# Two groups of heads in half a bank, a causal mask carried by 43 contraction rows, and a feed-forward in pairs of blocks

## The chip, the cores and the metric

The kernel runs on one core of a Trainium2 chip. The time is device microseconds of one execution, the median of several. A core has TensorE (PE, matmuls into eight PSUM banks of 128 partitions x 512 fp32), VectorE (DVE), ScalarE (ACT), GpSimd (POOL, which doesn't touch PSUM) and SyncE (SP), whose queue issues every DMA here.

## The reference

One gated cross-attention layer and one gated expert layer over x of 8 batches x 256 tokens x 128 channels:

```
xn  = layernorm(x)
y   = softmax(causal(q k^T)) v + softmax(qc kc^T) vc      # 16 heads of 8 channels; kc, vc from ctx (256 x 64)
x1  = x + tanh(g_xattn) * (y Wp + bp)
xn2 = layernorm(x1)
w   = route(xn2)                                          # 4 of 16 experts, chosen in 2 of 4 groups
out = x1 + tanh(g_ffn) * sum_e w[e] * (silu(xn2 Wg_e) * (xn2 Wu_e)) Wd_e     # 64 hidden channels an expert
```

In the self-attention a query token attends to keys at or before it; the others count as minus infinity ahead of the softmax. The cross-attention has no mask.

## The kernel before, in words

All 8 batches go through the same steps, and the steps of neighbouring batches overlap. No scheduler decides at build time: `ORDERS` holds one list of words for each engine (`max:3:11` is chunk 11 of batch 3), and an engine runs its list strictly in order. What one step needs of another engine is a semaphore wait at its head.

Scores are made twice. Queries and keys are split into three bf16 parts, and stacked along the contraction: rows 0 to 71 of `q_stack` and `k_stack` give fp32-like products of one head, and row 72 (`SHIFT_ROW`) holds minus the row's maximum in `q_stack` and 1.0 in `k_stack`. The stacks are written through DRAM (`part_scr`) by DMAs of 24 rows each, three for q and three for k, of each batch and each kind (CROSS, SELF); three slots of stacks rotate.

- `max_chunk` (L704, L701): scores with queries on the partitions, 512 columns to a bank, two banks; DVE takes the maximum of each row (`take_max`, L859, 28 a batch). In SELF chunks a matmul of `ident_b` with the constant `causal` (L695) first writes 0 or -1e30 into the diagonal blocks, and the score matmuls add to it.
- `exp_chunk` (L717): scores with keys on the partitions, with the shift row, two banks; ACT writes their exponentials to `probs` (L627, 28 a batch). In SELF chunks POOL then sets the positions of later keys to 0 (`mask`, L541, 12 a batch).
- `weigh_values` (L737, `pv` in the orders): four heads side by side, each in 32 of the 128 output partitions: 8 values, a sum of weights, and 23 zero columns of `v_ext`. One group of four heads fills half of `pv_bank` (256 queries), so a kind's 16 heads fill two banks one after the other.
- `evacuate_pv` (L633, ACT) copies each full bank; PE transposes it in four 128x128 blocks (`y`, L775); `merge` (DVE, L866 and L874) divides by the sums; `add_kinds` (POOL, L548) adds the two kinds. All of this happens four times a batch, the adding twice.
- Then `yT`, `wp`, the residual, the second layernorm, `logits`, the routing (`route`, DVE, 18 small steps), and its weights transposed (`combT`), sent to DRAM and spread over all partitions by DMA (`cout`, `cin`).
- The feed-forward works in 8 blocks of 128 hidden channels. Two banks rotate, each with a block's gates in one half and its ups in the other (`gate_up`, L805, L806). ACT takes the tanh of the gates (L643), DVE makes `f_gate` (`swish`, L939) and times the ups (`times_up`, L946), POOL multiplies with the routing weights (`combine`, L555, `fhc` in the orders), and `down` (L814) adds the eight blocks up in the next bank of the two.

An fp32 matmul stands in the trace as two instructions. Ten small uses of PE share one bank, `misc`, strictly in turn.

## Time and profile before

| | us |
|---|---|
| median of 3 runs (382.36 to 383.38) | 382.51 |
| profiled execution, its own time | 381.71 |
| its span in the trace | 379.9 |
| PE busy, 3200 matmuls | 346.4 |
| DVE busy | 270.2 |
| ACT busy | 206.0 |
| POOL busy | 200.6 |

The profile page gives each engine's busy time as the union of its instructions. A matmul's interval lasts from its start until its last column is through the array, so the intervals of matmuls that follow each other overlap: what a matmul costs PE is the distance to the next one's start, read from a timeline. In a timeline several instructions in a row of the same kind are one row with their count.

```
PE   1759989999999999999999999999999989997594
DVE  2127588686898789888787778777788785566751
ACT  1321247688767645676467645864576557643020
POOL 5935031564870889079525992185704830955313
```

These are tenths of busy time in 40 slices of 9.5 us. PE is full from 60 us to 340 us. Ahead of that the first batches come through loads, splits and DMAs; behind it the last batch's routing and feed-forward stand alone.

### The profile page before, as it was taken

The numbers are of one execution on the slowest core, as the hardware profiler recorded it, in microseconds if no ns is written. First come the engines' busy times: TensorE is split into PE (matmuls) and PEld (weight loads), VectorE is DVE, ScalarE is ACT, GpSimd is POOL, SyncE is SP. The second block draws the span as 40 slices with busy tenths as digits, with TensorE's granted clock in tenths as the row PEclk, the third lists the DMA queues.
The fourth block names the chain that finished last, engine by engine and source line by source line (L and its number), as shares of the span: only waits on it lengthen the run. The fifth ranks groups of instructions, "written<-read, shape, count | busy, mean of one in ns | idle before, by whom it ended". The sixth has DMA issues, their size and how long they took to land.

```text
span 379.9 us, 8947 instructions
## 1 busy us (share of the span) xinstructions
PE 346.4 (91%) x3200; PEld 250.6 (66%) x3200; DVE 270.2 (71%) x742; ACT 206.0 (54%) x442; POOL 200.6 (53%) x304
## 2 busy tenths in 40 slices
PE   1759989999999999999999999999999989997594
PEld 0423556676777787677876788678867867865454
DVE  2127588686898789888787778777788785566751
ACT  1321247688767645676467645864576557643020
POOL 5935031564870889079525992185704830955313
PEclk9999999999999999999999999999999999999789
DMA  3265144463344742494315422644044204105060
GB/s 92 83 201 155 59 126 144 142 205 117 94 127 129 159 145 60 138 172 126 112 47 127 129 89 93 150 91 117 17 133 96 43 14 94 23 18 110 2 125 16
DMA packets 31325, 39.13 MB, mean 103 GB/s; under 512 B 2832, under 2 KB 28592, under 8 KB 28848
## 3 DMA queue, kind: packets, MB, share of 16 engines
q1 hardware_dynamic: 31280, 38.55, 37.9%
q8 instruction: 26, 0.43, 0.4%
q14 instruction: 19, 0.16, 0.1%
HBM read 30.89 MB, written 7.47 MB: 101 GB/s over the span
## 4 chain that ended last, share of the span: by engine, by line
PE 77%; DVE 8%; DMA 5%; SPq 3%; ACT 2%; issue 2%; POOL 2%; POOLq 0%; ACTq 0%
PE bank L737 13%; PE bank L717 12%; PE bank L704 8%; PE bank L805 7%; PE bank L806 6%; PE bank L814 6%; PE bank L701 5%; DMA k_stack<-part_scr 5%; PE bank L695 4%; PE bank L775 3%; PE bank L756 2%; PE bank L743 2%; SPq L444 2%; PE bank L758 1%; PE bank L765 1%
## 5 line engine op out<-in xcount | busy, mean ns | idle before, releaser
L859 DVE TENSOR_REDUCE row_max<-bank 128x2 f32<-128x512 f32 (+1 forms) x224 | 149.3, 686 | 46.4 <-PE bank L704 27.4
L627 ACT ACTIVATE probs<-bank 128x512 f32<-128x512 f32 x224 | 128.6, 596 | 54.7 <-PE bank L717 44.7
L717 PE MATMUL bank<-q_stack,k_stack 73*128 73x256 bf16 (+1 forms) x512 | 80.5, 259 | 0.4 <-ACT probs L627 0.3
L541 POOL TENSOR_SCALAR_AFFINE_SELECT probs<-probs 128x256 f32<-128x256 f32 (+1 forms) x96 | 44.7, 482 | 35.7 <-ACT probs L627 35.2
L737 PE MATMUL bank<-probs,v_ext 128*32 128x256 f32 (+1 forms) x1024 | 61.7, 358 | 0.0
L555 POOL TENSOR_TENSOR f_h<-f_h,comb 128x256 f32<-128x256 f32 x64 | 45.3, 725 | 22.1 <-DMA comb<-c_scr 11.3
L704 PE MATMUL bank<-k_stack,q_stack 72*128 72x256 bf16 x256 | 50.1, 290 | 5.4 <-DMA k_stack<-part_scr 4.0
L717 PEld LDWEIGHTS bank<-q_stack,k_stack 73*128 73x128 bf16 x512 | 42.3, 98 | 14.9 <-ACT probs L627 5.7
L396 POOL TENSOR_TENSOR rest<-proj,part 128x512 f32<-128x512 f32 x14 | 16.2, 1157 | 59.9 <-ACT part L604 59.9
L805 PE MATMUL bank<-xn2T,w_pairs_sb 128*128 128x256 f32 x128 | 40.7, 400 | 2.3 <-DVE f_h L946 1.4
L737 PEld LDWEIGHTS bank<-probs,v_ext 128*32 128x32 f32 x1024 | 26.7, 109 | 23.2 <-issue 8.9
L643 ACT ACTIVATE f_tanh<-bank 128x256 f32<-128x256 f32 x64 | 24.3, 383 | 30.7 <-PE bank L806 29.5
L814 PE MATMUL bank<-w_down,f_h 128*128 128x128 f32 x256 | 37.8, 284 | 1.7 <-DVE f_h L946 1.3
L806 PE MATMUL bank<-xn2T,w_pairs_sb 128*128 128x256 f32 x128 | 38.7, 384 | 0.0
L704 PEld LDWEIGHTS bank<-k_stack,q_stack 72*128 72x128 bf16 x256 | 22.7, 101 | 22.3 <-DVE row_max L859 10.9
L701 PE MATMUL bank<-k_stack,q_stack 72*128 72x128 bf16 x384 | 37.4, 220 | 0.0
L939 DVE SCALAR_TENSOR_TENSOR f_gate<-f_tanh,bank 128x256 f32<-128x256 f32 x64 | 26.6, 415 | 14.4 <-ACT f_tanh L643 14.4
L814 PEld LDWEIGHTS bank<-w_down,f_h 128*128 128x128 f32 x256 | 32.5, 193 | 3.9 <-DVE f_h L946 1.7
L701 PEld LDWEIGHTS bank<-k_stack,q_stack 72*128 72x128 bf16 x384 | 30.1, 98 | 6.3 <-issue 0.8
L695 PE MATMUL bank<-causal,ident_b 128*128 128x256 bf16 (+1 forms) x96 | 30.4, 316 | 2.1 <-DVE row_max L859 1.4
L806 PEld LDWEIGHTS bank<-xn2T,w_pairs_sb 128*128 128x128 f32 x128 | 24.8, 194 | 3.6
L946 DVE TENSOR_TENSOR f_h<-f_gate,bank 128x256 f32<-128x256 f32 x64 | 26.4, 416 | 1.0
(103 smaller groups left out, 431.0 us busy)
## 6 DMA issues: line engine op xcount, KB each, us to landing
q_stack<-part_scr SPq DMA_DIRECT2D x48, 192.0 KB
k_stack<-part_scr SPq DMA_DIRECT2D x48, 192.0 KB
comb<-c_scr SPq DMA_DIRECT2D x16, 512.0 KB, 6.9
part_scr<-part SPq DMA_DIRECT2D x48, 128.0 KB, 3.2
x_in<-in_x SPq DMA_DIRECT2D x8, 128.0 KB, 2.8
w_pairs_sb<-in_w_pairs SPq DMA_DIRECT2D x1, 1024.0 KB, 7.0
out<-y_out SPq DMA_DIRECT2D x8, 128.0 KB, 2.4
ctx_in<-in_ctxT SPq DMA_DIRECT2D x8, 64.0 KB, 3.5
```

What stands on the lines that cost most here:

```text
L541: nc.gpsimd.affine_select(out=p, in_=p, compare_op=ALU.is_ge, fill=0.0, base=0, pattern=[[0, nh], [1, 128]], channel_multiplier=-1).then_i ...
L555: nc.gpsimd.tensor_tensor(at, at, comb[:, j, :], ALU.mult).then_inc(f_hc_done, 1)
L627: nc.scalar.activation(probs[:, seq % NP, :], exp_bank[s % 2][:, :], ACT.Exp).then_inc(exp_done, 1)
L695: pe.matmul(ps[:, :, keys - 128:keys], ident_b[:, :], causal[:, 0:nh, :], start=True, stop=False)
L701: last = pe.matmul(ps[:, n, kt * 128:(kt + 1) * 128], q, k_stack[0:STACK, s, kind, h, kt * 128:(kt + 1) * 128], start=False, stop=n == nh ...
L704: last = pe.matmul(ps[:, n, :], q, k_stack[0:STACK, s, kind, h, :], start=n == 0, stop=n == nh - 1)
L717: last = pe.matmul(ps[:, n, :], k_stack[0:STACK + 1, b % SLOTS, kind, h, kt * 128:(kt + 1) * 128], q_stack[0:STACK + 1, b % SLOTS, kind, h ...
L737: last = pe.matmul(pv_bank[32 * n:32 * n + VW, col + q0:col + T], v_ext[:, b % 2, kind, kt, 4 * g4 + n, :], p, start=kt == 0, stop=kt == N ...
L805: pe.matmul(gu_bank[use % 2][:, 0:T], w_gate[:, e0], xn2T[:, :], start=True, stop=True)
L806: pe.matmul(gu_bank[use % 2][:, T:2 * T], w_up[:, e0], xn2T[:, :], start=True, stop=True).then_inc(gu_ready, 1)
L814: last = pe.matmul(gu_bank[use % 2][:, n * 128:(n + 1) * 128], f_h[:, j, n * 128:(n + 1) * 128], w_down[:, j, :], start=j == 0 and n == 0, ...
L859: nc.vector.tensor_reduce(row_max[:, kind, qt, h0:h0 + nh], max_bank[k % 2][:, :].rearrange("p (h k) -> p h k", h=nh), AX.X, ALU.max).then ...
```

## The change

1. **Masks.** `causal`, `ident_b`, their matmul and POOL's `mask` are gone. Rows 73 to 115 of both SELF stacks hold constants `tri_q` and `tri_k` (43 rows, three tokens to a row), whose products add at most 2^-30 in size where the key is at or before the query, and -2^22 or less where it is later (all factors are powers of two). Matmuls on a diagonal block contract over 116 rows, the others over 72 or 73 as before. For that the exponential chunks of keys 0 to 127, one matmul of 256 queries a head before, are two matmuls of 128 (L731); all other widths stay. The maxima's diagonal matmuls now also read the shift row, so each load of a SELF `q_stack` is followed by a DMA that clears it (`zero_row`). Six DMAs (`tri`) place the constants in the three slots, of 43 rows x 8 KB each.
2. **Values.** Groups 2n and 2n+1 take the even and the odd heads of the same eight. The odd group reads its 32 columns of `v_ext` 16 further left, so that its values come out in partitions 16 to 31 of each strip, where the even group adds zeros. A kind's 16 heads fill one bank. Copy, transposes, merge run twice a batch, the adding once.
3. **Feed-forward.** Gates of two blocks fill `gate_bank`, ups of two blocks `up_bank`; neither has a second one. `gates_of` waits for the swish of the pair before, `ups_of` for its product. Tanh, swish, product and combine work on 512 columns, 4 a batch instead of 8. `down` writes into `gate_bank`.
4. All five orders are written anew for these steps.

```diff
+ROW_TOKENS = 3
+ROWS = (128 + ROW_TOKENS - 1) // ROW_TOKENS
+MASKED = STACK + 1 + ROWS
+AT = (2.0 ** 40, 2.0 ** -12, 2.0 ** -64)
+FROM = (2.0 ** -70, 2.0 ** -18, 2.0 ** 34)
+LATER = 2.0 ** 92
...
     'pe': '''
-        gu:6:2 y:7:3 gu:6:3 yT:7 wp:7 gu:6:4 gu:6:5 gu:6:6 gu:6:7 xn2T:7 logits:7 down:6 down:6:1 down:6:2 down:6:3
-        down:6:4 down:6:5 down:6:6 combT:7 down:6:7 gu:7 gu:7:1 gu:7:2 gu:7:3 gu:7:4 gu:7:5 gu:7:6 gu:7:7 down:7
...
+        ga:6:1 up:6:1 yT:7 wp:7 ga:6:2 up:6:2 ga:6:3 up:6:3 xn2T:7 logits:7 down:6 down:6:1 down:6:2 down:6:3 down:6:4
+        down:6:5 down:6:6 down:6:7 combT:7 ga:7 up:7 ga:7:1 ga:7:2 up:7:1 ga:7:3 up:7:2 up:7:3 down:7 down:7:1
...
+            def place_masks(s):
+                if s == 0:
+                    sp.wait_ge(const_made, 3)
+                else:
+                    sp.wait_ge(tri_in[0], 32)
+                for st, tri in ((q_stack, tri_q), (k_stack, tri_k)):
+                    first = tri[:, 0:T].unsqueeze(1).broadcast_to([ROWS, H, T])
+                    src = first if s == 0 else st[SHIFT_ROW + 1:MASKED, 0, SELF]
+                    sp.dma_start(st[SHIFT_ROW + 1:MASKED, s, SELF], src).then_inc(tri_in[s], 16)
...
+                if kind == SELF and qk == 0:
+                    if b == 0:
+                        sp.wait_ge(const_step, 4)
+                    sp.dma_start(q_stack[SHIFT_ROW:SHIFT_ROW + 1, b % SLOTS, SELF], zero_row[:, :]).then_inc(stack_in[b % SLOTS][SELF], 16)
...
+                    nc.gpsimd.memset(at_q[:, :, c:c + 1], -AT[c]).then_inc(const_step, 1)
+                    nc.gpsimd.memset(at_k[:, :, c:c + 1], FROM[c]).then_inc(const_step, 1)
+                pool.wait_ge(const_step, 4 + 2 * ROW_TOKENS)
...
-            def mask(b, m):
-                s = CROSS_C2 + m
-                _, kt, h0, nh, q0 = S2_CHUNKS[s]
-                pool.wait_ge(exp_done, b * NC2 + s + 1)
-                p = probs[:, (b * NC2 + s) % NP, :].rearrange("p (h q) -> p h q", h=nh)[:, :, 0:128]
-                nc.gpsimd.affine_select(out=p, in_=p, compare_op=ALU.is_ge, fill=0.0, base=0,
-                                        pattern=[[0, nh], [1, 128]], channel_multiplier=-1).then_inc(mask_done, 1)
...
-                if kind == SELF:
-                    pe.matmul(ps[:, :, keys - 128:keys], ident_b[:, :], causal[:, 0:nh, :], start=True, stop=False)
                 for n in range(nh):
-                    h = h0 + n
-                    q = q_stack[0:STACK, s, kind, h, qt * 128:(qt + 1) * 128]
+                    q, key = q_stack[:, s, kind, h0 + n, qt * 128:(qt + 1) * 128], k_stack[:, s, kind, h0 + n, :]
                     if kind == SELF:
-                        for kt in range(keys // 128):
-                            last = pe.matmul(ps[:, n, kt * 128:(kt + 1) * 128], q, k_stack[0:STACK, s, kind, h, kt * 128:(kt + 1) * 128],
-                                             start=False, stop=n == nh - 1 and kt == keys // 128 - 1)
+                        for kt in range(qt + 1):
+                            rows_used = MASKED if kt == qt else STACK
+                            last = pe.matmul(ps[:, n, kt * 128:(kt + 1) * 128], q[0:rows_used], key[0:rows_used, kt * 128:(kt + 1) * 128],
+                                             start=n == 0 and kt == 0, stop=n == nh - 1 and kt == qt)
...
-                    last = pe.matmul(ps[:, n, :], k_stack[0:STACK + 1, b % SLOTS, kind, h, kt * 128:(kt + 1) * 128],
-                                     q_stack[0:STACK + 1, b % SLOTS, kind, h, q0:T], start=n == 0, stop=n == nh - 1)
+                    h = h0 + 2 * n
+                    key, q = k_stack[:, b % SLOTS, kind, h, kt * 128:(kt + 1) * 128], q_stack[:, b % SLOTS, kind, h, :]
+                    if kind == SELF:
+                        for qt in range(kt, NQ):
+                            rows_used = MASKED if kt == qt else STACK + 1
+                            last = pe.matmul(ps[:, n, qt * 128 - q0:(qt + 1) * 128 - q0], key[0:rows_used], q[0:rows_used, qt * 128:(qt + 1) * 128],
+                                             start=n == 0 and qt == kt, stop=n == nh - 1 and qt == NQ - 1)
...
-                if kind == SELF:
-                    pe.wait_ge(mask_done, b * SELF_C2 + 3 * g4 + 3)
-                if g % 2 == 0:
-                    ge(pe, pv_copied, b * 4 + g // 2)
-                col = (g % 2) * T
+                if g4 == 0:
+                    ge(pe, pv_copied, b * 2 + kind)
+                col = g4 // 2 * T
...
+                        at = h * VW - VW // 2 * (g4 % 2)
+                        last = pe.matmul(pv_bank[32 * n:32 * n + VW, col + q0:col + T],
+                                         v_ext[:, b % 2, kind, kt].rearrange("p h v -> p (h v)")[:, at:at + VW], p,
+                                         start=g4 % 2 == 0 and kt == 0, stop=g4 % 2 == 1 and kt == NQ - 1, tile_position=(0, 32 * n))
...
+            def hidden(b, j, bank_of, w):
+                for n in range(2):
+                    e0 = (2 * j + n) * 128
+                    last = pe.matmul(bank_of[:, n * T:(n + 1) * T], w[:, e0:e0 + 128], xn2T[:, :], start=True, stop=True)
+                return last
+
+            def gates_of(b, j):
                 if j == 0:
                     misc_evacuated(pe, "xn2T", b)
                     if b == 0:
                         pe.wait_ge(w_experts, 32)
-                use = b * GU_USES + j
-                ge(pe, gu_free, use - 1)
-                e0 = slice(j * 128, (j + 1) * 128)
-                pe.matmul(gu_bank[use % 2][:, 0:T], w_gate[:, e0], xn2T[:, :], start=True, stop=True)
-                pe.matmul(gu_bank[use % 2][:, T:2 * T], w_up[:, e0], xn2T[:, :], start=True, stop=True).then_inc(gu_ready, 1)
+                    ge(pe, out_made, b)
+                ge(pe, f_gate_done, b * GP + j)
+                hidden(b, j, gate_bank, w_gate).then_inc(gates_ready, 1)
+
+            def ups_of(b, j):
+                ge(pe, ups_free, b * GP + j)
+                hidden(b, j, up_bank, w_up).then_inc(ups_ready, 1)
...
             def down(b, j):
-                use = b * GU_USES + NB
                 if j == 0:
-                    pe.wait_ge(gu_free, use - 1)
-                pe.wait_ge(f_hc_done, b * NB + j + 1)
+                    pe.wait_ge(f_gate_done, b * GP + GP)
+                pe.wait_ge(f_hc_done, b * GP + j // 2 + 1)
...
-                nc.vector.scalar_tensor_tensor(out=f_gate[:, j % 2], in0=f_tanh[:, j % 2], scalar=1.0, in1=gu_bank[(b * GU_USES + j) % 2][:, 0:T],
+                dve.wait_ge(f_tanh_done, b * GP + j + 1)
+                ge(dve, ups_free, b * GP + j)
+                nc.vector.scalar_tensor_tensor(out=f_gate[:, :], in0=f_tanh[:, :], scalar=1.0, in1=gate_bank[:, :],
...
+                dve.wait_ge(ups_ready, b * GP + j + 1)
```

**The orders, place 1: PE at the first SELF maxima of batch 0.** L695 is the mask matmul, L701 (after: L711) the SELF score matmuls, L770 (L787) the transposes of `shift`, L704 (L714) CROSS maxima, L717 (L734) CROSS exponentials. Before, and then after:

```order
L760 MATMUL bank<-xnT,w_model_sb 128x256
L695 MATMUL bank<-causal,ident_b 128x512
L701 MATMUL bank<-k_stack,q_stack 128x128 x4
L695 MATMUL bank<-causal,ident_b 128x512
L701 MATMUL bank<-k_stack,q_stack 128x128 x4
L770 MATMUL bank<-ident,row_max 16x128 x2
L695 MATMUL bank<-causal,ident_b 128x512
L701 MATMUL bank<-k_stack,q_stack 128x128 x4
```

```order
L777 MATMUL bank<-xnT,w_model_sb 128x256
L714 MATMUL bank<-k_stack,q_stack 128x256 x2
L787 MATMUL bank<-ident,row_max 16x128 x2
L711 MATMUL bank<-k_stack,q_stack 128x128 x16
L734 MATMUL bank<-q_stack,k_stack 128x256 x2
L711 MATMUL bank<-k_stack,q_stack 128x128 x8
L734 MATMUL bank<-q_stack,k_stack 128x256 x6
```

The mask matmuls between the groups of four are gone, and the transposes of `shift` have moved ahead of the SELF maxima.

**Place 2: DVE from the end of batch 7's routing to the feed-forward behind it.** L931 (after: L955) makes the last routing weight, L946 (L972) is the product with the ups, L985 (L1011) writes batch 6's output, L939 (L964) is the swish. Before, and then after:

```order
L928 RECIPROCAL r_sum<-r_sum 128x2
L931 SCALAR_TENSOR_TENSOR r_w<-r_sel,gate,r_sum 128x32
L946 TENSOR_TENSOR f_h<-f_gate,bank 128x256
L985 TENSOR_TENSOR y_out<-bank,x 128x256
L939 SCALAR_TENSOR_TENSOR f_gate<-f_tanh,bank 128x256
L946 TENSOR_TENSOR f_h<-f_gate,bank 128x256
```

```order
L952 RECIPROCAL r_sum<-r_sum 128x2
L955 SCALAR_TENSOR_TENSOR r_w<-r_sel,gate,r_sum 128x32
L1011 TENSOR_TENSOR y_out<-bank,x 128x256
L964 SCALAR_TENSOR_TENSOR f_gate<-f_tanh,bank 128x512
L972 TENSOR_TENSOR f_h<-f_gate,bank 128x512
L964 SCALAR_TENSOR_TENSOR f_gate<-f_tanh,bank 128x512
```

Before, the last product of batch 6 stands behind the routing of batch 7; after, it stands ahead of it.

**Place 3: SP while batch 0's SELF stacks are loaded.** L433 (after: L440) stores parts, L444 (L451) loads stacks, L448 (L459) sets a shift row, L430 places masks, L455 clears the row. Before, and then after:

```order
L411 DMA x_in<-in_x 128x2x128 [waits res_done,xn_done,misc_ready]
L412 DMA ctx_in<-in_ctxT 64x256
L433 DMA part_scr<-part 128x2x256 [waits split_cross]
L444 DMA q_stack<-part_scr 24x1x4096 [waits part_out_self]
L444 DMA q_stack<-part_scr 24x1x4096 x2
L444 DMA k_stack<-part_scr 24x1x4096 [waits part_out_self]
L444 DMA k_stack<-part_scr 24x1x4096 x2
L444 DMA q_stack<-part_scr 24x1x4096 [waits part_out_cross]
L444 DMA q_stack<-part_scr 24x1x4096 x2
L433 DMA part_scr<-part 128x2x256 [waits split_self]
L448 DMA q_stack<-shiftT 1x16x256 [waits misc_free]
```

```order
L430 DMA q_stack<-tri_q 43x16x256 [waits const_made]
L430 DMA k_stack<-tri_k 43x16x256
L451 DMA k_stack<-part_scr 24x1x4096 [waits part_out_self]
L451 DMA k_stack<-part_scr 24x1x4096 x2
L440 DMA part_scr<-part 128x2x256 [waits split_cross]
L408 DMA x_in<-in_x 128x2x128 [waits res_done,xn_done,misc_ready]
L409 DMA ctx_in<-in_ctxT 64x256
L451 DMA q_stack<-part_scr 24x1x4096 [waits part_out_self]
L451 DMA q_stack<-part_scr 24x1x4096 x2
L455 DMA q_stack<-zero_row 1x16x256 [waits const_step]
L440 DMA part_scr<-part 128x2x256 [waits split_cross]
```

After, two mask DMAs stand ahead of batch 0's SELF keys, and one that clears the shift row follows the SELF queries; batch 1's CROSS queries, ahead of the shift row before, are not among the rows: they come behind it.

## Rows read from the trace of the kernel before

**Rows 1.** The page: busy time of each engine, and the chain that ended last

```profile
PE 346.4 (91%) x3200; PEld 250.6 (66%) x3200; DVE 270.2 (71%) x742; ACT 206.0 (54%) x442; POOL 200.6 (53%) x304
...
PE 77%; DVE 8%; DMA 5%; SPq 3%; ACT 2%; issue 2%; POOL 2%; POOLq 0%; ACTq 0%
```

**Rows 2.** Windows: from:to, length, busy (x instructions) by engine, PEclk, DMA share, GB/s

```profile
0.00:45.00 45.00, 28.37 (x84) 14.66 (x85) 16.79 (x42) 11.36 (x25) 23.43 (x34) 1.00 0.41 124
...
45.00:60.00 15.00, 13.00 (x133) 8.27 (x131) 12.87 (x21) 8.05 (x17) 3.81 (x3) 1.00 0.39 116
...
100.00:140.00 40.00, 40.00 (x421) 29.28 (x419) 34.69 (x91) 26.20 (x58) 25.16 (x36) 1.00 0.49 132
...
340.00:380.00 40.00, 27.95 (x154) 20.66 (x142) 20.73 (x69) 7.39 (x19) 14.47 (x22) 0.91 0.30 61
...
60.00:340.00 280.00, 277.09 (x2842) 207.05 (x2844) 219.84 (x612) 179.15 (x383) 158.90 (x245) 1.00 0.39 105
```

**Rows 3.** Groups by form: shapes, count | busy us, mean ns | idle before

```profile
L695 PE MATMUL bank<-causal,ident_b 128*128 128x256 bf16 x64 | 17.6, 276 | 1.5 <-DVE row_max L859 1.4
...
L695 PE MATMUL bank<-causal,ident_b 128*128 128x512 bf16 x32 | 12.7, 398 | 0.6 <-DMA k_stack<-part_scr 0.5
...
L775 PE MATMUL bank<-ident,y_raw 128*128 128x128 f32 x128 | 19.7, 276 | 0.0
```

**Rows 4.** Timeline of PE, 133.0 to 134.8 us: start us, us, what, count

```profile
133.03 0.38 PE L695 MATMUL bank<-causal,ident_b 128*128 128x512 bf16 x1
133.25 0.39 PE L701 MATMUL bank<-k_stack,q_stack 72*128 72x128 bf16 x4
133.47 0.61 PE L775 MATMUL bank<-ident,y_raw 128*128 128x128 f32 x4
133.91 0.39 PE L717 MATMUL bank<-q_stack,k_stack 73*128 73x128 bf16 x4
134.14 0.27 PE L695 MATMUL bank<-causal,ident_b 128*128 128x256 bf16 x1
134.25 0.39 PE L701 MATMUL bank<-k_stack,q_stack 72*128 72x128 bf16 x4
134.48 0.38 PE L717 MATMUL bank<-q_stack,k_stack 73*128 73x256 bf16 x2
134.70 0.27 PE L695 MATMUL bank<-causal,ident_b 128*128 128x256 bf16 x1
```

**Rows 5.** Groups by form on DVE, ACT and POOL

```profile
L859 DVE TENSOR_REDUCE row_max<-bank 128x2 f32<-128x512 f32 x192 | 127.8, 685 | 37.4 <-PE bank L704 27.4 <-PE bank L701 7.7
...
L939 DVE SCALAR_TENSOR_TENSOR f_gate<-f_tanh,bank 128x256 f32<-128x256 f32 x64 | 26.6, 415 | 14.4 <-ACT f_tanh L643 14.4
...
L946 DVE TENSOR_TENSOR f_h<-f_gate,bank 128x256 f32<-128x256 f32 x64 | 26.4, 416 | 1.0
...
L866 DVE RECIPROCAL recip<-bank 128x16 f32<-128x16 f32 x32 | 8.0, 251 | 6.6 <-PE bank L775 6.4
...
L874 DVE TENSOR_TENSOR y_self<-bank,recip 128x128 f32<-128x128 f32 x16 | 4.7, 292 | 0.6
...
L627 ACT ACTIVATE probs<-bank 128x512 f32<-128x512 f32 x224 | 128.6, 596 | 54.7 <-PE bank L717 44.7 <-PE bank L737 8.7
...
L541 POOL TENSOR_SCALAR_AFFINE_SELECT probs<-probs 128x512 f32<-128x512 f32 x32 | 20.3, 633 | 4.8 <-ACT probs L627 4.7
...
L402 POOL TENSOR_TENSOR part<-rest,part 128x512 bf16<-128x512 f32 x14 | 16.2, 1157 | 0.4
```

**Rows 6.** Timeline of the end: start us, us, what

```profile
368.51 5.51 POOL L555 TENSOR_TENSOR f_h<-f_h,comb 128x256 f32<-128x256 f32 x8 [9.18 <-DMA comb<-c_scr]
...
372.53 3.84 PE L814 MATMUL bank<-w_down,f_h 128*128 128x128 f32 x32 [1.26 <-DVE f_h L946]
...
376.40 0.42 DVE L985 TENSOR_TENSOR y_out<-bank,x 128x256 f32<-128x256 f32 x1 [3.60 <-PE bank L814]
```

**Rows 7.** Chain in order of time: a wait for a stack of batch 1

```profile
48.66 5.33 DMA k_stack<-part_scr
```

More of the change, by code:

```diff
@@ L48 @@
 for g in range(H // 4):
-    S2_CHUNKS += [(CROSS, kt, 4 * g + hp, 2, 0) for kt in range(NQ) for hp in (0, 2)]
+    S2_CHUNKS += [(CROSS, kt, first_head(g) + 2 * hp, 2, 0) for kt in range(NQ) for hp in (0, 2)]
     S2_GROUP += [g] * 4
 for g in range(H // 4):
-    S2_CHUNKS += [(SELF, 0, 4 * g, 2, 0), (SELF, 0, 4 * g + 2, 2, 0), (SELF, 1, 4 * g, 4, 128)]
+    S2_CHUNKS += [(SELF, 0, first_head(g), 2, 0), (SELF, 0, first_head(g) + 4, 2, 0), (SELF, 1, first_head(g), 4, 128)]
     S2_GROUP += [H // 4 + g] * 3
@@ L337, in build @@
         bank = [stack.enter_context(nc.psum_tensor(f"bank{n}", [128, 512], FP32)) for n in range(8)]
-        max_bank, exp_bank, pv_bank, gu_bank, misc = bank[0:2], bank[2:4], bank[4], bank[5:7], bank[7]
+        max_bank, exp_bank, pv_bank, gate_bank, up_bank, misc = bank[0:2], bank[2:4], bank[4], bank[5], bank[6], bank[7]
         w_first, w_rows, w_experts = sem("w_first"), sem("w_rows"), sem("w_experts")
@@ L343, in build @@
         const_step, const_made = sem("const_step"), sem("const_made")
+        tri_step, tri_in = sem("tri_step"), [sem(f"tri_in{s}") for s in range(SLOTS)]
         v_clear_step, v_cleared = sem("v_clear_step"), sem("v_cleared")
@@ L472, in _ @@
                     place_constants()
+                elif what == "tri":
+                    place_masks(n)
                 elif what == "experts":
@@ L490, in _ @@
             sp.wait_ge(ones_in, 16 * SLOTS)
+            for s in range(SLOTS):
+                sp.wait_ge(tri_in[s], 32)
         @block.gpsimd
@@ L573, in _ @@
                     split_step(nc.gpsimd, b, n, 2)
-                elif what == "mask":
-                    mask(b, n)
                 elif what == "yadd":
-                    add_kinds(b, n)
+                    add_kinds(b)
                 elif what == "rstd2":
@@ L688, in max_chunk @@
                     stack_here(pe, b, kind)
[L689 to L690 removed]
+                if b < SLOTS and k == CROSS_C1:
+                    pe.wait_ge(tri_in[b], 32)
                 ge(pe, max_taken, b * NC1 + k - 1)
@@ L715, in exp_chunk @@
                 for n in range(nh):
-                    h = h0 + n
-                    last = pe.matmul(ps[:, n, :], k_stack[0:STACK + 1, b % SLOTS, kind, h, kt * 128:(kt + 1) * 128],
-                                     q_stack[0:STACK + 1, b % SLOTS, kind, h, q0:T], start=n == 0, stop=n == nh - 1)
+                    h = h0 + 2 * n
[5 more added lines that the diff above has]
+                                             start=n == 0 and qt == kt, stop=n == nh - 1 and qt == NQ - 1)
+                    else:
+                        last = pe.matmul(ps[:, n, :], key[0:STACK + 1], q[0:STACK + 1], start=n == 0, stop=n == nh - 1)
                 last.then_inc(exp_scores, 1)
@@ L771, in misc_use @@
                 elif what == "y":
-                    pe.wait_ge(pv_copied, b * 4 + n + 1)
+                    pe.wait_ge(pv_copied, b * 2 + n + 1)
                     for qt in range(NQ):
-                        for g in range(2):
-                            last = pe.transpose(misc[:, (qt * 2 + g) * 128:(qt * 2 + g + 1) * 128],
-                                                y_raw[:, n % 2, g * T + qt * 128:g * T + (qt + 1) * 128], ident[:, :])
+                        for p in range(2):
+                            last = pe.transpose(misc[:, (qt * 2 + p) * 128:(qt * 2 + p + 1) * 128],
+                                                y_raw[:, n, p * T + qt * 128:p * T + (qt + 1) * 128], ident[:, :])
                 elif what == "yT":
-                    pe.wait_ge(y_added, 2 * b + 2)
+                    pe.wait_ge(y_added, b + 1)
                     last = transposes(y)
```

430 lines of the change are left out of this document (205 added, 225 removed).

## The prediction

> **What bounds the kernel now.** I read the page's busy times and its chain first, then the busy time by stage, then PE's timeline inside the full stage, and the waits of the other engines last. PE is busy for 346.4 of 379.9 us and holds 77% of the chain that ended last, DVE 8% [rows 1]. By stage it is three kernels [rows 2]. Up to 60 us the first batches' stacks are made and loaded, and PE is busy for 28 of the first 45 us and 13 of the next 15, while DVE is busy for 12.9 of those 15: it paces the maxima of batch 0. From 60 to 340 us PE is busy for 277.1 of 280 us. From 340 us on the last batch's routing and feed-forward stand alone, at a mean granted clock of 0.91, with PE busy for 28 of 40 us in short pieces between other engines.
>
> PE's busy time is a union of overlapping intervals, so I take costs from starts instead. In the piece of timeline in [rows 4] the starts follow without a hole: the mask matmul of 512 columns holds PE for 0.22 us, the one of 256 for 0.11, four score matmuls of 128 columns for 0.22 to 0.23 (0.055 each), two of 256 for 0.22 (0.11 each), four fp32 transposes for 0.44 (0.11 each). What is taken from PE's stream in the full stage is taken from the time, if nothing else is as near to its limit. DVE is the next: 34.7 of 40 us in its fullest window [rows 2]. ACT has 179 and POOL 159 of the 280.
>
> The Trainium skill ("Perfetto Trace Analysis", Identifying the Most-Contended Engine) calls matmul busy time a bad measure of how close PE is to its limit and asks for the busy share of weight loads. That share is 207.1 of 280 us here [rows 2], so by the rule PE would have room; the starts in [rows 4] say that it has none where I looked, and the measurement decides.
>
> **The change part by part.**
>
> *Mask matmuls.* 32 of 512 columns and 64 of 256 go [rows 3]: 32 x 0.22 + 64 x 0.11 = 14.1 us of PE's stream. One batch in eight lies in the start, where DVE paces and nothing is gained, so 12.3 us count. The 43 more contraction rows cost nothing: with 128 rows (L695) and with 73 (L717) 256 columns take the same 0.11 us [rows 4].
>
> *Exponential chunks of keys 0 to 127.* 64 chunks of two matmuls of 256 columns become four of 128, 128 more instructions. By [rows 4] both forms fill the same 0.22 us, so the likeliest price is 0. It can't be below that, as no column goes. Above, each of the 128 added matmuls, with its own load of weights, could cost as much as a whole one of 256 columns, 0.11: 14 us. L701 is the nearest row, so I stay at 0.
>
> The Trainium skill ("TensorE: Matmul & The Clock Gate", Back-to-back issue gap) speaks against this edit: in a stream of loads and matmuls it gives some 81 ns for each matmul of 128 columns. By it a chunk would take 324 ns instead of 220, 6.7 us over the 64 chunks. The 384 matmuls of L701 have the same shape and show 55 ns, so the row stands in the sum.
>
> *Values and transposes.* The value matmuls keep their number, width and order of accumulation. The transposes of `y` halve, from 128 to 64 [rows 3]: 64 x 0.11 = 7.0 us. The last batch's four in the end lie in a stretch where PE waits anyway, 0.5; I count 6.5. `pv_bank` is handed over twice a batch instead of four times, which takes two waits of PE for ACT's copy away; I cost that at nothing, since other work is queued there.
>
> *Masks on POOL.* 96 instructions go, up to 0.633 us each [rows 5]. POOL is busy for 159 of 280 us and off the path. But each of 32 SELF groups of values waits for its last mask. At 0.63 us each that is at most 20 us of PE's wait; the order fills it with other matmuls as far as the starts show. I cost it at nothing, with 10 us (half of them exposed) as the end on the fast side.
>
> *DVE.* 64 swishes and 64 products of 256 columns, 0.415 us each, become 32 and 32 of 512. The only PSUM operation of 512 columns on DVE takes 0.685 [rows 5]: 53.2 us become 43.8. Merges: 32 x (0.251 + 0.292) = 17.4 us become 16 x (0.27 + 0.42) = 11.0, with the reciprocal of 32 columns just above that of 16, and the product of 256 columns as L946. In all 15.8 us less, 13.8 of it in the full stage. DVE falls by 6% there, PE's stream by 18.8 of some 280, 7%: the order of the engines stays.
>
> *Feed-forward in the full stage.* PE's columns stay. The new thing is that gates j+1 wait for swish j. The cycle is four fp32 pieces of 256 columns, 0.88 by twice the 0.11 of [rows 4], 0.17 for the last to come through (0.61 less 0.44 in the same rows), a tanh of 512 columns as L627, 0.60, and a swish, 0.69 [rows 5], with some 0.1 of hand-overs: 2.4 us. PE's order has some 3 us of other work between two pairs of gates there (for batch 5: five exponential chunks, a group of values, the ups, a transpose pair: 1.1 + 1.0 + 0.9 + 0.2), so nothing is paid.
>
> *The end.* Before, POOL's eight products run from 368.51 to 374.02, PE's last block is done at 376.37 [rows 6]. After, four of 512 columns follow the same transfer of routing weights. The one row of that width is L402, 1.157 us [rows 5], so 4.6 us instead of 5.5. That is 0.9. Before, PE ended 2.35 us behind POOL's last product; after, two of eight `down` blocks stand behind it, eight matmuls of 0.12 (3.84 / 32), 1.0 us: another 1.3. This holds if the gates are done in time. Four rounds of 2.4 us, two products of 0.69 that DVE's order puts ahead of a swish, and the last ups and product, 0.9 + 0.7, are 12.6 us from the first gates; order place 2 gives them an earlier start, since batch 6's last product stands ahead of batch 7's routing: a product on DVE (0.42), one on POOL (0.69) and four matmuls of 0.12 are 1.6 us that no longer stand between the routing and the gates. The merge and the addition ahead of it are wider by some 0.4 us and have one copy and transpose step fewer, which I cost at nothing. I take -2.2 for the end.
>
> *The start.* POOL makes the new constants with eleven small instructions instead of four, ahead of batch 1's normalisation, and SP issues two mask DMAs ahead of batch 0's SELF keys (order place 3). A pair of them moves 2 x 43 x 8 KB = 0.69 MB; the last of a stack's three loads, 0.58 MB in all, landed 5.33 us after its issue [rows 7], so a pair costs the DMA engines up to 6.4 us, and there are three pairs by the third batch. Below: 0, since SELF stacks of batch 0 are needed only after its 16 CROSS maxima, 16 x 0.69 = 11 us of DVE. I take +1.0, near the lower end, as the engines are busy for 0.39 to 0.41 of that time [rows 2]. Each later SELF load carries one DMA more of 8 KB; it is ahead of need by a batch.
>
> Sum against the profiled execution of 381.7 us: -12.3 - 6.5 - 2.2 + 1.0 = -20.0, so 361.7. Its time lies 0.8 under the median of the runs shown, which makes 362.5; I say 362.
>
> **The rivals.**
>
> *DVE takes the pace.* For it: 34.7 of 40 us in [rows 2], with the maxima unchanged. Then the full stage shrinks by DVE's 13.8 us instead of 18.8: 367. Against it: DVE's chain share of 8%, and its idle time ahead of the maxima ends mostly on PE (27.4 of 37.4 us) [rows 5].
>
> *Waits go too.* The 10 us of exposed mask waits above come on top: 352. For it: four engines lose work at once, and the bank `misc` has 16 fewer turns. Against: PE's starts have no holes in [rows 4].
>
> *The start pays.* The masks delay batch 0's or 1's stacks by a full pair, 6.4 us instead of 1.0: 368.
>
> *The split is not free.* Its price falls between 6.7 us by the page's rule and the bound of 14: 369 to 376.
>
> *Slower: PE stands before its single gate bank.* Were the tanh to stand behind one exponential (0.60) and the swish behind one maximum (0.69), the cycle is 3.7 us, and PE, which runs in order, would wait up to 1.3 us ahead of each of 32 pairs: 41 us, 403 in all. With half of that it is 382. It decides from a mean wait of 20 / 32 = 0.63 us a pair. Against it: both queues pass several instructions in the 3 us of cover. The Trainium skill ("Perfetto Trace Analysis", Optimizing Tensor Performance) has this rule: independent groups of matmuls should rotate through banks, so that an evacuation lies beside the next group. The change breaks it for gates and ups; no row of before shows an unrotated bank.
>
> **How the numbers follow.** The forecast, 358 to 366, has 0.5; DVE's pace 0.15; waits gone too 0.18; the start 0.07; the split 0.05; the gate bank 0.05, of which 0.03 is slower than before. The range 351 to 372 leaves out the gate bank, most of the split and the fastest of the waits. Faster by over 0.3% (1.1 us, about what can be told from no change) is everything but the gate bank and a sliver of the split: 0.95; within 0.3%: 0.02; slower: 0.03.
>
> **What would show it.** PE's busy windows stay full from 60 us on and the full stage is shorter by 19 us; the new 128-column matmuls in the exponentials start 0.055 us apart; SELF score matmuls of 116 rows as well. DVE's swish and product take 0.69 us at 512 columns and its total falls from 270.2 to some 254 us. PE's waits ahead of gates (their line's idle time) stay under 0.2 us a pair, and the end's combine and `down` last 5.6 us from the landing of the weights. The forecast is wrong if the starts in the full stage have holes that end on DVE's maxima (rival one), on swish or product (the gate bank), or if the first 60 us grow by more than 3 us.

## The result, and the profile after

| | before | after |
|---|---|---|
| median of 4 runs each, us | 382.53 | 444.22 (441.83 to 445.92) |
| ratio, 95% interval | | 1.160 [1.155, 1.166] |
| profiled execution, us | 381.71 | 441.83 |
| its span, us | 379.9 | 440.1 |

The forecast was 362. The kernel became 16% slower. Of all executions below, one of e6 and one of e8 ran about 2% slower than the others of the same kernel, and the medians leave them out. The page of the changed kernel, busy time and granted clock in 40 slices of 11 us, and the chain:

```profile
PE 336.6 (76%) x3168; PEld 244.2 (55%) x3168; DVE 259.9 (59%) x646; ACT 195.4 (44%) x394; POOL 152.9 (35%) x176
...
PE   2669004980199703999999999999999999998766
...
PEclk9999999995599955999999999999999999999989
DMA  3230053421146210436414715552372332143250
...
PE 48%; DMA 19%; SPq 14%; DVE 8%; POOL 6%; issue 2%; ACT 2%; POOLq 0%; ACTq 0%; DVEq 0%
```

PE does less work than in [rows 1], as forecast, but has three holes ahead of 175 us, and DMA and SP's queue hold a third of the chain instead of 8%. Two milestones cut each profile in three, the start of the last value matmul of batch 1 and of batch 7:

| us | start | six batches | end | span |
|---|---|---|---|---|
| before | 108.2 | 232.0 | 39.7 | 379.9 |
| after | 182.2 | 216.8 | 41.1 | 440.1 |
| difference | +74.0 | -15.2 | +1.4 | +60.2 |

The full stage gained nearly what was forecast (18.8 us for seven batches, so 16.1 for six). All of the loss but 1.4 us is in the start. Its first hole, from PE's timeline:

```profile
45.20 0.58 PE L787 MATMUL bank<-ident,row_max 128*16 128x128 f32 x2 [0.88 <-DVE row_max L885]
70.01 1.04 PE L711 MATMUL bank<-k_stack,q_stack 116*128 116x128 bf16 x8 [24.22 <-DMA q_stack<-zero_row]
```

SP's queue at the same time shows why. The second column is how long issuing took:

```profile
23.93 0.73 SPq L430 DMA_DIRECT2D q_stack<-tri_q  x1
24.69 16.51 SPq L430 DMA_DIRECT2D k_stack<-tri_k  x1
41.25 17.51 SPq L451 DMA_DIRECT2D k_stack<-part_scr  x3
58.80 0.45 SPq L440 DMA_DIRECT2D part_scr<-part  x1
...
60.43 2.08 SPq L451 DMA_DIRECT2D q_stack<-part_scr  x3
```

A DMA is issued in about 0.7 us. The second mask DMA took 16.51, and the three loads behind it 17.51, so batch 0's SELF queries were issued at 60.4 us. What moved meanwhile (windows, columns as in [rows 2]):

```profile
30.00:40.00 10.00, 9.26 (x34) 4.86 (x34) 8.25 (x17) 1.04 (x3) 6.26 (x7) 1.00 0.07 22
40.00:56.00 16.00, 4.92 (x14) 2.20 (x13) 2.01 (x4) 1.68 (x4) 0.00 (x0) 1.00 0.07 22
```

0.07 of sixteen engines is about one, and it moves 22 GB/s. At that rate the pair's 0.70 MB takes 32 us; in the trace the rate holds from 28 to 58 us. The semaphore increments by which the two DMAs report say the same: each DMA makes two, one right behind its issue (25.1 and 41.6 us) and one as it lands (44.2 and 60.7 us). The other two holes are the copies into slots 1 and 2 (98 to 120 and 156 to 172 us), in the SELF score matmuls' row:

```profile
L711 PE MATMUL bank<-k_stack,q_stack 116*128 116x128 bf16 x256 | 35.9, 238 | 67.7 <-DMA k_stack<-part_scr 43.2 <-DMA q_stack<-zero_row 24.2 <-DVE row_max L885 0.4
```

Its 67.7 us of idle time are nearly the whole loss of the start. The holes also cost clock (below).

The Trainium skill ("DMA: Bandwidth & Descriptors", Why a DMA increments its semaphore by 16 and not by 1) has the rule: a DMA goes on the largest number of engines, up to 16, that divides the slowest dimension (leaving out those of size 1) of its source and of its destination. 43 is prime and above 16, so that number is 1. The windows agree (a share of 0.07), and so do the increments, one each as the data land. The prediction didn't weigh it.

The terms that the forecast had sized, in the rows after:

```profile
L964 DVE SCALAR_TENSOR_TENSOR f_gate<-f_tanh,bank 128x512 f32<-128x512 f32 x32 | 21.9, 683 | 11.3 <-ACT f_tanh L654 11.0
...
L569 POOL TENSOR_TENSOR f_h<-f_h,comb 128x512 f32<-128x512 f32 x32 | 40.1, 1271 | 58.8 <-DMA comb<-c_scr 42.7
...
L817 PE MATMUL bank<-xn2T,w_pairs_sb 128*128 128x256 f32 x256 | 69.8, 401 | 4.8 <-DVE f_gate L964 3.6
...
L731 PE MATMUL bank<-q_stack,k_stack 116*128 116x128 bf16 x256 | 33.0, 223 | 0.0
```

### The profile page after: what moved, and what is told of

It is laid out like the page before. It is cut to its first block, busy times and chain, and to the rows that moved or that the text cites. A ratio compares the mean times of both kernels' runs of the same rounds, so it can differ in the third digit from the quotient of the medians.

```text
span 440.1 us, 8571 instructions
## 1 busy us (share of the span) xinstructions
PE 336.6 (76%) x3168; PEld 244.2 (55%) x3168; DVE 259.9 (59%) x646; ACT 195.4 (44%) x394; POOL 152.9 (35%) x176
## 4 chain that ended last, share of the span: by engine, by line
PE 48%; DMA 19%; SPq 14%; DVE 8%; POOL 6%; issue 2%; ACT 2%; POOLq 0%; ACTq 0%; DVEq 0%
DMA k_stack<-part_scr 14%; PE bank L817 10%; PE bank L753 9%; SPq L451 8%; PE bank L734 6%; PE bank L838 5%; SPq L430 4%; PE bank L711 4%; PE bank L714 4%; PE bank L731 3%; DMA q_stack<-shiftT 2%; DVE row_max L885 2%; DMA comb<-c_scr 2%; DMA part_scr<-part 2%; POOL xn L548 1%
## 5 line engine op out<-in xcount | busy, mean ns | idle before, releaser
L711 PE MATMUL bank<-k_stack,q_stack 116*128 116x128 bf16 (+1 forms) x384 | 39.5, 235 | 68.1 <-DMA k_stack<-part_scr 43.2
L711 PEld LDWEIGHTS bank<-k_stack,q_stack 116*128 116x128 bf16 (+1 forms) x384 | 29.7, 106 | 74.9 <-DMA k_stack<-part_scr 43.5
L569 POOL TENSOR_TENSOR f_h<-f_h,comb 128x512 f32<-128x512 f32 x32 | 40.1, 1271 | 58.8 <-DMA comb<-c_scr 42.7
L714 PE MATMUL bank<-k_stack,q_stack 72*128 72x256 bf16 x256 | 50.5, 291 | 5.8 <-DMA k_stack<-part_scr 3.3
L817 PEld LDWEIGHTS bank<-xn2T,w_pairs_sb 128*128 128x128 f32 x256 | 45.6, 197 | 12.9 <-DVE f_gate L964 5.2
L734 PE MATMUL bank<-q_stack,k_stack 73*128 73x256 bf16 x256 | 47.8, 282 | 2.3 <-DMA q_stack<-shiftT 1.5
L731 PE MATMUL bank<-q_stack,k_stack 116*128 116x128 bf16 (+1 forms) x384 | 36.2, 223 | 0.0
L714 PEld LDWEIGHTS bank<-k_stack,q_stack 72*128 72x128 bf16 x256 | 21.4, 101 | 25.0 <-DVE row_max L885 11.9
L838 PEld LDWEIGHTS bank<-w_down,f_h 128*128 128x128 f32 x256 | 32.2, 191 | 3.4 <-POOL f_h L569 1.7
L731 PEld LDWEIGHTS bank<-q_stack,k_stack 116*128 116x128 bf16 (+1 forms) x384 | 28.2, 100 | 6.0 <-ACT probs L639 1.6
L734 PEld LDWEIGHTS bank<-q_stack,k_stack 73*128 73x128 bf16 x256 | 21.9, 101 | 12.9 <-issue 5.5
L964 DVE SCALAR_TENSOR_TENSOR f_gate<-f_tanh,bank 128x512 f32<-128x512 f32 x32 | 21.9, 683 | 11.3 <-ACT f_tanh L654 11.0
```

What stands on the lines that cost most here:

```text
L569: nc.gpsimd.tensor_tensor(at, at, comb[:, 2 * j:2 * j + 2, :], ALU.mult).then_inc(f_hc_done, 1)
L711: last = pe.matmul(ps[:, n, kt * 128:(kt + 1) * 128], q[0:rows_used], key[0:rows_used, kt * 128:(kt + 1) * 128], start=n == 0 and kt == 0, ...
L714: last = pe.matmul(ps[:, n, :], q[0:STACK], key[0:STACK], start=n == 0, stop=n == nh - 1)
L731: last = pe.matmul(ps[:, n, qt * 128 - q0:(qt + 1) * 128 - q0], key[0:rows_used], q[0:rows_used, qt * 128:(qt + 1) * 128], start=n == 0 an ...
L734: last = pe.matmul(ps[:, n, :], key[0:STACK + 1], q[0:STACK + 1], start=n == 0, stop=n == nh - 1)
L817: last = pe.matmul(bank_of[:, n * T:(n + 1) * T], w[:, e0:e0 + 128], xn2T[:, :], start=True, stop=True)
```

## The experiments

Theory A: the loss is the mask DMAs, because their 43 rows go on one engine. Rival B, where a run could bear it out: size, alignment or amount of the DMAs, or the new orders of the start. Each run's ratio is against runs of the kernel before on the same chip (medians 382.2 to 382.4). Times are medians. e1 to e4 ran on one chip, e5 to e8 on a second, e9 to e12 on a third.

| run | us | ratio, 95% | start | six batches | end |
|---|---|---|---|---|---|
| e1, 48 rows | 374.17 | 0.978 [0.972, 0.984] | 113.9 | 216.0 | 41.4 |
| e2, 32 + 11 rows | 377.34 | 0.986 [0.978, 0.993] | 118.3 | 215.6 | 41.4 |
| e3, before + dead DMAs of 43 | 469.73 | 1.227 [1.215, 1.239] | 198.5 | 232.6 | 39.5 |
| e4, before + dead DMAs of 48 | 397.4 | 1.038 [1.033, 1.044] | 124.2 | 232.5 | 39.4 |
| e5, 48 rows, copies earlier | 374.07 | 0.980 [0.977, 0.984] | 115.1 | 219.2 | 41.5 |
| e6, e5 with a new end | 374.21 | 0.981 [0.977, 0.985] | 116.0 | 216.0 | 40.5 |
| e7, no mask DMAs | 371.2 | 0.970 [0.968, 0.973] | 110.3 | 215.4 | 42.1 |
| e8, before, no masks | 371.49 | 0.972 [0.970, 0.975] | 106.6 | 222.4 | 39.2 |
| e9, 47 rows | 451.34 | 1.183 [1.178, 1.188] | 191.3 | 217.0 | 42.5 |
| e10, 44 rows | 374.45 | 0.980 [0.974, 0.986] | 111.6 | 219.4 | 41.2 |
| e11, before, split | 382.5 | 1.002 [0.999, 1.005] | 108.0 | 233.0 | 39.4 |
| e12, before, no mask matmuls | 375.66 | 0.983 [0.977, 0.989] | 108.6 | 225.8 | 40.9 |

**e1, e9, e10: the number of rows.** The stacks and constants get a few more rows, everything else stays.

```diff
-MASKED = STACK + 1 + ROWS
+PLACED = 48                      # e9: 47, e10: 44
+MASKED = STACK + 1 + PLACED
```

> The changed kernel with the masks padded from 43 to 48 rows (five rows of zeros in k_stack), all orders unchanged. Theory A, a DMA whose outer dimension is 43 runs on one of the 16 DMA engines: with 48 rows it runs on 16, the three holes of PE (43 to 74, 99 to 120, 148 to 172 us in the trace of after) close, and the time falls from 444 to 362 to 372 us, below before. Rival B, copies within SBUF or this much data are slow as such, or SP is stopped by the number of packets: 12% more bytes, 440 to 450 us. Rival C, the new orders themselves put the holes there: 430 to 445 us.

> The changed kernel with 47 mask rows instead of 43: 9% more mask bytes, still a prime number of rows, and one row short of the 48 that took 374 us. Theory A (a DMA is cut over as many engines as divide its rows, and over one where the rows are prime): one engine carries each mask DMA, the copies last 47/43 as long, and the time is 444 to 452 us. Rival B (what counts is that 43 rows are awkward in size or alignment, and 48 more nearly so): a time between, nearer to 374.

> The changed kernel with 44 mask rows. Theory A: 44 rows go on 11 engines, so a copied pair takes 11/16 of the rate and 44/48 of the bytes of the 48-row kernel's, 1.33 times as long, some 1 us a pair: 374 to 377 us, between the 48-row kernel and the one with DMAs of 32 and 11 rows (377.3). Rival B (size or alignment): near 444.

One row between 47 and 48 is worth 77 us; 44 rows take what 48 take, within the intervals. Neither the amount nor a size near 43 explains that. Which divisor counts is told by the traces' semaphore increments from DMAs: a pair of mask DMAs makes 4 with 43 or 47 rows, 24 with 44, 32 with 48, so 2, 12 and 16 for each DMA. Where it is under 16, the first comes right behind the issue, ahead of the data; 1, 11 and 16 are left, the largest divisors up to 16 of 43 or 47, 44 and 48. A rule such as "a multiple of 4" would not give 11. SP's queue of e1 at the place shown above, and then the windows of e1 and of e9:

```profile
23.93 0.71 SPq L431 DMA_DIRECT2D q_stack<-tri_q  x1
24.68 0.65 SPq L431 DMA_DIRECT2D k_stack<-tri_k  x1
29.09 2.30 SPq L452 DMA_DIRECT2D k_stack<-part_scr  x3
```

```profile
24.00:40.00 16.00, 12.13 (x43) 5.96 (x42) 10.41 (x20) 3.02 (x7) 6.25 (x7) 1.00 0.75 184
```

```profile
30.00:40.00 10.00, 9.26 (x34) 4.90 (x32) 7.93 (x15) 1.04 (x3) 6.25 (x7) 1.00 0.07 22
```

The same DMAs with more rows, and the loads behind them, move 184 GB/s instead of 22. e1 beats the kernel before by 2.2%.

**e2: the same 43 rows, cut.** Each mask DMA is issued as one of 32 and one of 11 rows; waits count four DMAs.

```diff
-sp.dma_start(st[SHIFT_ROW + 1:MASKED, s, SELF], src).then_inc(tri_in[s], 16)
+for lo, hi in ((0, 32), (32, ROWS)):
+    sp.dma_start(st[SHIFT_ROW + 1 + lo:SHIFT_ROW + 1 + hi, s, SELF], src[lo:hi]).then_inc(tri_in[s], 16)
```

> The changed kernel with each mask DMA of 43 rows cut into one of 32 and one of 11 rows, same bytes and rows. Theory A: 11 is prime, so the second piece still runs on one engine, with 11/43 of the work: about 4 of 16 us for a broadcast DMA and 3.4 of 13 us for a copy, so three quarters or more of the loss goes, 368 to 385 us. Rival B (bytes or packets): no change, 440 to 450 us.

The contraction over 116 rows and the bytes are those of the changed kernel, and 67 us are gone: it is the cut of the DMA alone. One premise of the expectation was wrong: the piece of 11 rows did not run on one engine. The four DMAs of a slot make 56 increments, 16 + 12 twice, so the 11 rows went on 11 engines. 11 is prime, but below 16.

**e3, e4: the DMAs alone, in the kernel before.** Six DMAs like the masks', into rows that nothing reads, at the places of the new order.

```diff
+tri:0 ahead of pd0:1, tri:0:1 ahead of kst:1:1, tri:0:2 ahead of kst:2:1
+sp.dma_start(st[SHIFT_ROW + 1:SHIFT_ROW + 1 + 43, s, SELF], src).then_inc(tri_in[s], 16)     # e4: 48
```

> The kernel before with its own orders and arithmetic, to which only the six mask DMAs of 43 rows are added, at the same places among SP's words, into rows 73 to 115 that nothing reads. Theory A: the DMAs alone carry the loss, through the loads queued behind them; 430 to 450 us. Rival C (the orders): 383 to 390 us.

> The same with 48 rows. Theory A: 382 to 386 us, the price of the mask DMAs when they use all engines. Rival B: as with 43 rows.

43 dead rows cost 87 us with none of the change's other parts; 48 cost 15. Both lie above what was expected (430 to 450 and 382 to 386). So even on 16 engines a pair is not free: batch 1's and 2's keys stand behind it, and in the old orders that costs far more than in the new ones (below). PE's first mask matmul in e4:

```profile
L712 PE MATMUL bank<-causal,ident_b 128*128 128x256 bf16 (+1 forms) x96 | 31.7, 330 | 13.3 <-DMA k_stack<-part_scr 11.2 <-DVE row_max L876 1.9
```

**e5, e6: can the 48-row kernel be made better?** e5 issues the copies ahead of the shift row that they stood behind; e6 also reorders the last feed-forward.

```diff
 sp:  -shd:0:1 tri:0:1   +tri:0:1 shd:0:1      -shd:1:1 tri:0:2   +tri:0:2 shd:1:1
 e6:  pe -down:6:7 combT:7 ga:7   +down:6:7 ga:7 combT:7   and   -ga:7:2 up:7:1 ga:7:3   +up:7:1 ga:7:2 up:7:2 ga:7:3
      dve -route:7:4 route:7:5 out:6   +out:6 route:7:4 route:7:5      act -combT_e:7 tanh:7   +tanh:7 combT_e:7
```

> The changed kernel with 48 mask rows (374.2 us in its own run) and, in SP's order, the two copies of the masks for slots 1 and 2 ahead of the shift row that they stood behind. Theory A (the mask DMAs set the start's loss): in the 48-row kernel SP stood from 55.5 to 61.4 us and from 84.8 to 93.5 us before shift rows, with the copies and the SELF keys behind them; issued ahead, the copies use that idle time and the keys come earlier. Batch 1's last values end about 4 us earlier (110 instead of 113.9), the time is 369 to 371. Rival B (the start's remaining +5.7 us against the kernel before lies in PE's and DVE's new orders, not in the masks): 373.5 to 375, unchanged.

> As the run before it, and the last feed-forward reordered: batch 6's output moved into the middle of batch 7's routing on DVE, the first gates of batch 7 on PE and their tanh on ACT ahead of the transpose of the routing weights, and ups 1 ahead of gates 2. Theory A (the chain gates, tanh, swish, gates on a single gate bank sets the end, with products of the ups in between): the gates start some 2 us earlier, but POOL then has to wait for the landing of the routing weights and needs 4 x 1.27 us behind it, so the end comes 1.0 to 1.5 us earlier. Rival B (the landing of the routing weights and POOL set the end already): no gain, within 0.3 us of the run before it.

e5's theory falls: slot 1's copies were issued 5.7 us earlier (56.28 instead of 61.97), and no time was gained: 374.07, with the start at 115.1 where 110 was expected. PE now waits longer for other transfers. The profiled execution of e5, 377.5 us, was the longest of its six, so its rows tell the place and not the price. The CROSS scores of e1 and of e5:

```profile
L715 PE MATMUL bank<-k_stack,q_stack 72*128 72x256 bf16 x256 | 50.6, 291 | 5.5 <-DMA k_stack<-part_scr 3.0 <-DVE row_max L886 2.2
```

```profile
L715 PE MATMUL bank<-k_stack,q_stack 72*128 72x256 bf16 x256 | 50.8, 292 | 9.5 <-DMA k_stack<-part_scr 6.1 <-DVE row_max L886 2.2 <-DMA q_stack<-part_scr 0.8
```

e6 gains nothing in the medians either (374.21), but its profile shows an end 1.0 us shorter than e5's (40.5 instead of 41.5), as expected, too little for these medians to tell. Its timeline tells what bounds the end. The rounds of the gate bank, and then POOL and the end:

```profile
358.44 1.99 PE L818 MATMUL bank<-xn2T,w_pairs_sb 128*128 128x256 f32 x8 [0.55 <-DVE f_gate L965]
...
360.98 1.99 PE L818 MATMUL bank<-xn2T,w_pairs_sb 128*128 128x256 f32 x8 [0.55 <-DVE f_gate L965]
...
363.56 4.94 POOL L570 TENSOR_TENSOR f_h<-f_h,comb 128x512 f32<-128x512 f32 x4 [14.78 <-DMA comb<-c_scr]
364.97 4.74 PE L839 MATMUL bank<-w_down,f_h 128*128 128x128 f32 x32 [2.00 <-POOL f_h L570]
369.75 0.42 DVE L1012 TENSOR_TENSOR y_out<-bank,x 128x256 f32<-128x256 f32 x1 [5.57 <-PE bank L839]
```

A round now takes 2.54 us, near the forecast 2.4, and the first three products are ready as the routing weights land. What bounds the end here is that landing and POOL behind it, without a pause. Counted from the start of the last value matmul, POOL starts at 31.6 us in e6 and at 31.5 in e1, so the gates ahead of the weights' transposes did not delay the landing; the last product is ready at 32.2 instead of 35.8, and the last output starts at 37.8 instead of 38.6.

**e7, e8, e12, e11: the sizes of the terms.** e7 takes the DMAs and the mask rows out of the changed kernel; e8 and e12 take masks out of the kernel before; e11 puts the split into it.

```diff
 e7:   place_masks(n) -> pass;  rows_used = STACK (maxima), STACK + 1 (exponentials)
 e8:   -pe.matmul(ps[:, :, keys - 128:keys], ident_b[:, :], causal[:, 0:nh, :], start=True, stop=False)
       -mask(b, n)   -pe.wait_ge(mask_done, b * SELF_C2 + 3 * g4 + 3)
 e12:  only the first line of e8
 e11:  +for lo, hi in ((0, 128), (128, 256)): pe.matmul(... q_stack[..., lo:hi] ...)      # SELF, keys 0 to 127
```

> The changed kernel with its orders, without the six mask DMAs; its SELF products contract over 72 or 73 rows, so causality is left out of the computation. What remains is everything but the placing of the masks. Theory A (the mask DMAs alone are the loss, 43 rows on one DMA engine): the time falls from 444 to 368 to 372, under the 48-row kernel's 374.2 by what its copies still cost; the end of batch 1's last values near 110 us. Rival B (part of the loss lies in the new orders of the start): 374 or more, with that milestone at 113 us or later.

> The kernel before without the 96 mask matmuls on PE and without POOL's 96 masks: causality is left out of the computation, all else stays. By the prediction's terms the mask matmuls are worth 12.3 us of PE's stream in the full stage and POOL's masks nothing: 370 (1.76 us a batch). If the waits of the value groups for POOL's masks were exposed, up to 10 us more: 360. If another engine (DVE) sets the pace of the full stage, less than half of it: 376 or more.

> The kernel before without its 96 mask matmuls; POOL's masks of the exponentials stay. The row maxima are then taken over later keys too, the output stays causal. With POOL's masks left out as well it was 371.9. Theory A (POOL's masks were free): 372, the mask matmuls alone bring all of it. Rival B (value groups waited for POOL's masks): 374 to 377, what is left being POOL's.

> The kernel before with the exponential chunks of keys 0 to 127 as four matmuls of 128 columns instead of two of 256, all else unchanged. The prediction's term: 0, within 0.3% of 382.5, since rows show 0.055 us for a matmul of 128 columns. By the page's rule of 81 ns for each: +6.7, 389. By the upper bound (each added matmul as much as one of 256): +14, 396.

e7 gives the change's gain free of its DMAs: 371.2. With e1 it prices the masks on 16 engines at 3 us, as does e5, from the same chip as e7 (2.9). For e8 and e12 the full stages stand side by side (e12, then e8; windows):

```profile
108.60:334.40 225.80, 222.11 (x2236) 168.38 (x2228) 182.78 (x533) 143.37 (x313) 130.84 (x202) 1.00 0.39 100
```

```profile
106.60:329.00 222.40, 221.56 (x2240) 168.25 (x2231) 180.17 (x531) 143.04 (x313) 98.37 (x129) 1.00 0.39 102
```

Without the mask matmuls PE stands idle for 3.7 us in six batches, without POOL's masks as well for 0.8. The waits in e12 end on DVE's maxima, merge and output (3.0 us in sum) and on POOL's normalisation (0.4), not on the value groups. So POOL's masks reach PE by a detour. One way, not shown step by step, is what stands behind them on POOL. Another is DVE: its busy time falls from 182.8 to 180.2 us as the masks go, nearly all of it in the routing's small steps, whose length goes with what POOL does beside them (in e12, e8 and before together, `r_pair` of 24 columns takes 0.185 us with POOL idle, six of them, 0.185 beside its masks alone, two, and 0.64 beside its products, five). The runs show the sum of the two and do not separate them. e12's profiled execution also had a stretch of low clock in the start, so I take POOL's share from this stage: 3.4 us between the two windows; the medians differ by 4.2, from two chips. e11 bounds the split's price: at most 0.5%, 1.9 us.

## Why the prediction was wrong, step by step

*The start is the step that failed.* The prediction's own sign of being wrong, the first 60 us growing by more than 3, came true. I priced a pair of mask DMAs by its bytes against the landing of one stack's loads [rows 7], at most 6.4 us a pair, and took +1.0. That assumes that a DMA of 43 rows uses the engines as one of 24 does. It doesn't: a load of 24 rows makes 9 increments, the first right behind its issue, so 8 engines carry it; one engine carries the 43 rows, a pair takes 32 us at 22 GB/s, SP's next issues stretch to 16.51 and 17.51 us, and each of the three pairs stops PE: +74.0 up to batch 1's values. It was not in a rival either: "the start pays" was bounded by the same 6.4. The new orders would have shown the place (order place 3: masks ahead of SELF keys); the shape 43x16x256 stood in it. On 16 engines the term would only have been too small: e1 starts 5.7 us late, e7, without the DMAs, 2.1, so 3.6 us are the masks', where 1.0 stood. That holds for the new orders only: at nearly the same places among the old ones the same six DMAs on 16 engines cost 16 us up to this milestone (e4 against before). Why so much more is open. The remaining 2.1 lie in the new orders and constants; I haven't separated them further.

*Mask matmuls.* 14.1 us of PE's stream and 12.3 counted. e12 shows 6.5 in the medians, e8, with POOL's masks gone, 10.7 (11.7 in its profile). By the same prices 10.6 fall in six batches (24 x 0.22 + 48 x 0.11). There PE's busy time fell from 229.7 to 222.1 (e12) and 221.6 (e8), 7.6 and 8.1 us, less than forecast, and in e12 its idle time grew from 2.3 to 3.7 us, since other waits took part of it. "Waits go too" was true in part: POOL's masks were worth some 3 us, though not where I had looked.

*The split* cost nothing that e11 can tell (1.002, at most 1.9 us). The profile's 0.055 us was right, and the 81 ns of the Trainium skill ("TensorE: Matmul & The Clock Gate", Back-to-back issue gap) was not borne out for this stream of loads and matmuls: by it e11 would have been 6.7 us longer. 43 contraction rows cost nothing either: two matmuls of L731 in a row start 0.055 us apart with 116 rows, as with 73 in e7 (0.056), and six batches take 216.0 us in e1 and 215.4 in e7.

*Values and transposes, DVE, the gate bank.* From e8 to e7, which differ in these parts, the split and the orders, six batches shrink by 7.0 us, where 5.3 were forecast (0.88 each), and PE remains the bound: 214.0 of 215.4 us. DVE's swish takes 0.683 against 0.69; its merges take 12.4 us in all, not 11.0. PE waited 4.8 us ahead of gates and ups in all, 0.1 of it in the full stage. Both rivals, DVE's pace and the gate bank, are out for the full stage.

*The end.* -2.2 was forecast, +1.4 came, in two parts. The forecast took the landing of the routing weights as given and cost the steps ahead of it at nothing. That was wrong by 2.8 us: counted from the start of the last value matmul, POOL starts on the landed weights at 28.3 us before [rows 6] and at 31.1 after (430.12). In the new order the last transposes of `y` start at 2.5 us instead of 1.2, behind gates, ups and `combT`; the last merge at 3.7 instead of 1.8, behind a swish and a product of batch 6; the residual at 7.3 instead of 4.9. From the landing on, 1.4 us were gained, not 2.2. There the product on POOL takes 1.271 us in the mean, not 1.157, and the gates and products come late: POOL is done with the first three at 433.95 and waits 0.70 for the last. Gates 2 and 3 of the last batch start 3.6 us apart, not 2.4, since DVE's order puts product 1 ahead of swish 2 and the ups it needs stand on PE behind gates 2 (it waits 2.16 us for them). The last rows:

```profile
426.17 1.99 PE L817 MATMUL bank<-xn2T,w_pairs_sb 128*128 128x256 f32 x8 [1.41 <-DVE f_gate L964]
...
429.81 1.99 PE L817 MATMUL bank<-xn2T,w_pairs_sb 128*128 128x256 f32 x8 [1.64 <-DVE f_gate L964]
430.12 3.83 POOL L569 TENSOR_TENSOR f_h<-f_h,comb 128x512 f32<-128x512 f32 x3 [14.50 <-DMA comb<-c_scr]
...
434.66 1.27 POOL L569 TENSOR_TENSOR f_h<-f_h,comb 128x512 f32<-128x512 f32 x1 [0.70 <-DVE f_h L972]
437.39 0.42 DVE L1011 TENSOR_TENSOR y_out<-bank,x 128x256 f32<-128x256 f32 x1 [2.81 <-PE bank L838]
```

Free of DMAs, the change and its orders gain 11 us (e7). Taking the masks out of the old kernel gains 10.7 (e8). The halved transposes and the wide feed-forward bring 7.0 in the full stage; the new start (+3.7 against e8) and the new end (+2.9) give nearly all of it back. So the forecast's 20 would not have been reached even with a good DMA shape; 374.2 would have been just above its range.

## What to carry to other kernels

Ahead of pricing a DMA by its bytes, look at its slowest dimensions: with 43 or 47 rows, primes above 16, one engine did all the work, with 11 or 44 rows 11, with 48 rows 16. Padding to 44 or 48 rows moves 2% or 12% more bytes and took 70 us off here. Look also at what is queued behind a long transfer, since SP's issues behind it stretched as well. And when work is taken from the busiest engine, compare all three parts of a profile: what the full stage gains, new orders can give back at both ends.
